# Where the value projections stand in a window-attention layer: between the q/k projections and the spread of the norms, with the five engines' orders set anew

## The reference, cut to what matters

```python
for i in range(6):
    x = attn_layer(shift_tokens(x), Wqkv[i], q_scale[i], k_scale[i], Wo[i]) + x
    x = ffn_layer(shift_tokens(x), ln_g[i], ln_b[i], W1[i], b1[i], W2[i], b2[i]) + x

def attn_layer(x, Wqkv, qs, ksc, Wo):        # 16 heads of 64
    q, k, v = split(x @ Wqkv)
    q, k = l2norm(q) * qs, l2norm(k) * ksc   # norm over the 64 features of a head
    q = q * cos * scale + rotate_half(q) * sin * scale
    k = k * cos / scale + rotate_half(k) * sin / scale
    # windows of 32 queries; keys and values of this window and the one before
    attn = softmax(8 * q k^T + mask)
    return (attn @ v) @ Wo
```

## Time and profile before

| | us |
|---|---|
| median of 3 runs | 2266.87 (2265.04 to 2267.53) |
| profiled execution, its time | 2274.98 |
| its span | 2273.2 |
| PE busy | 2019.9 (89%) |
| DVE busy | 1615.8 (71%) |
| ACT busy | 1093.3 (48%) |
| POOL busy | 891.1 (39%) |
| mean granted TensorE clock | 0.962 |

### The profile page before, as it was taken

The page is one execution under the profiler, slowest core; times in us unless marked ns, Lnnn a source line. Parts: engine busy times, 40 slices in busy tenths (PEclk is TensorE's granted clock), DMA queues, the critical chain, the costliest instruction groups (busy, mean ns, idle before and its releaser), DMA issues.

```text
span 2273.2 us, 84305 instructions
## 1 busy us (share of the span) xinstructions
PE 2019.9 (89%) x35280; PEld 1310.9 (58%) x35280; DVE 1615.8 (71%) x3316; ACT 1093.3 (48%) x1911; POOL 891.1 (39%) x1166
## 2 busy tenths in 40 slices
PE   6989896789998999979999799999799998899996
PEld 2333332466665666656666566766566765666664
DVE  5556645678876788866878677878687876777872
ACT  2333332355554555544555455646355654455553
POOL 0000001445544545443545353545354544444540
PEclk9999998899998999989999999999999998999996
DMA  1000100545555655454656455556465545555550
GB/s 58 5 9 5 51 0 11 82 80 81 83 88 100 93 82 84 78 101 84 95 82 89 98 85 81 91 84 87 86 104 79 91 82 94 89 89 81 83 87 25
DMA packets 72441, 168.15 MB, mean 74 GB/s; under 512 B 16496, under 2 KB 23408, under 8 KB 71408
## 3 DMA queue, kind: packets, MB, share of 16 engines
q0 software_dynamic: 36864, 100.71, 33.1%
q1 hardware_dynamic: 35456, 65.55, 11.1%
HBM read 20.45 MB, written 1.05 MB: 9 GB/s over the span
## 4 chain that ended last, share of the span: by engine, by line
PE 61%; DVE 15%; DMA 11%; issue 9%; POOL 2%; ACT 1%; SPq 1%; DVEq 0%; POOLq 0%; ACTq 0%
PE ps L922 13%; DMA big<-big 9%; PE ps L955 8%; PE ps L844 6%; PE ps L933 4%; PE ps L1009 4%; PE ps L992 4%; PE ps L979 3%; DVE big L743 3%; DVE big L740 3%; PE ps L1029 3%; PE ps L1022 3%; PE ps L1065 2%; POOL big L425 2%; PE ps L865 2%
## 5 line engine op out<-in xcount | busy, mean ns | idle before, releaser
L425 POOL DMA_DIRECT2D big<-big x768 | 607.5, 1494 | 93.7 <-DVE big L743 80.3
L922 PE MATMUL ps<-big,wn_sb 128*128 128x256 f32 x1536 | 404.7, 401 | 42.1 <-DMA wn_sb<-in_wn 22.2
L493 ACT ACTIVATE big<-ps 128x512 f32<-128x512 f32 x384 | 228.2, 597 | 399.7 <-PE ps L922 393.5
L922 PEld LDWEIGHTS ps<-big,wn_sb 128*128 128x128 f32 x1536 | 280.4, 195 | 119.8 <-issue 35.5
L751 DVE TENSOR_TENSOR big<-big,ps 128x512 f32<-128x512 f32 x384 | 243.7, 681 | 122.5 <-PE ps L945 81.9
L740 DVE TENSOR_TENSOR big<-ps,tab 128x512 f32<-128x512 f32 x384 | 258.5, 682 | 46.8 <-ACT big L493 46.8
L506 ACT ACTIVATE big<-ps 128x512 f32<-128x512 f32 x192 | 114.7, 597 | 358.9 <-PE ps L955 358.9
L756 DVE TENSOR_REDUCE top<-ps 128x8 f32<-128x512 f32 x192 | 123.3, 684 | 223.6 <-PE ps L979 223.6
L416 POOL TENSOR_TENSOR big<-big 128x512 f32<-128x512 f32 x96 | 121.8, 1269 | 357.8 <-ACT big L510 357.8
L743 DVE TENSOR_TENSOR big<-ps,tab 128x512 f32<-128x512 f32 x384 | 257.7, 681 | 0.0
L1065 PE MATMUL ps<-big,wo_sb 128*128 128x256 f32 x768 | 217.1, 386 | 1.9 <-issue 1.9
(11 more groups left out here) (146 smaller groups left out, 3119.9 us busy)
## 6 DMA issues: line engine op xcount, KB each, us to landing
big<-big POOLq DMA_DIRECT2D x768, 128.0 KB, 4.8
big<-big SPq DMA_DIRECT2D x96, 256.0 KB, 3.7
big<-big SPq DMA_DIRECT2D x96, 192.0 KB, 3.9
wn_sb<-in_wn SPq DMA_DIRECT2D x6, 1536.0 KB, 7.6
wo_sb<-in_wo SPq DMA_DIRECT2D x6, 512.0 KB, 5.2
w_sb<-in_w SPq DMA_DIRECT2D x6, 341.0 KB, 3.9
w_sb<-in_w SPq DMA_DIRECT2D x6, 192.0 KB, 4.9
big<-in_x SPq DMA_DIRECT2D x8, 128.0 KB, 2.2
```

What stands on the lines that cost most here:

```text
L425: eng.dma_start(rot[to:to + 32, at:at + 4, :], src[32 * r:32 * r + 32], accum_op=ALU.add).then_inc(added[i], 16)
L493: eng.activation(sq[:, two, :], ps[:, i % 2, :].rearrange("p (a t) -> p a t", a=2), ACT.Square).then_inc(sq_d, 1)
L922: mm = eng.matmul(ps[:, k % 2, a * T:a * T + T], wn_sb[:, u * P:u * P + P], sT, start=True, stop=True)
```

## The change

The four lists are replaced, and three waits follow the new use of banks 0 and 1: projections, values, spread norms. `V0` and `V1` now wait for `d6` and `d7`. `R0` waits for the copy `v2` (and, as before, for `N6`), `R1` for `v3`. The next iteration's `k0` waits for `H6` and `k1` for `H7`, in place of the wait for the copies. In the lists `k0` comes ahead of `S0`; `V0` to `V3` stand behind `W3`; on ACT the Gelu step `F4` comes ahead of `n0`, and `v0` to `v3` between `n0` and `F5`. The instructions that the program writes out are the same ones.

```diff
         PE_PLAN = [(x_[0], int(x_[1:])) for x_ in """
-            S0 k0 k1 F1 S1 k2 k3 T0 g0 T1 F2 k4 k5 W0 W1 g1 g2 k6 T2 k7 U0 T3 g3 W2 W3 U1 F4 O0 O1 O2 U2 O3 U3
-            F5 R0 R1 O4 R2 O5 R3 O6 R4 F6 R5 R6 O7 F7 R7 V0 V1 V2 V3""".split()]
+            k0 S0 k1 F1 k2 F2 S1 T0 k3 T1 k4 g0 g1 W0 W1 k5 T2 k6 T3 F4 k7 U0 U1 g2 g3 W2 W3 V0 V1 V2 V3 F5 O0
+            R0 O1 U2 R1 R2 O2 F6 U3 O3 O4 R3 R4 O5 F7 R5 R6 O6 O7 R7""".split()]
         ACT_PLAN = [(x_[0], int(x_[1:])) for x_ in """
-            s0 s1 x0 F1 s2 s3 t0 F2 t1 s4 s5 x1 s6 t2 s7 u0 t3 F3 n0 u1 F4 u2 u3 F5 v0 v1 v2 v3""".split()]
+            s0 F1 s1 s2 x0 F2 t0 s3 t1 x1 s4 s5 F3 t2 t3 s6 s7 F4 n0 v0 u0 v1 u1 v2 v3 F5 u2 u3""".split()]
         DVE_PLAN = [(x_[0], int(x_[1:])) for x_ in """
-            X0 X1 D0 D1 c0 c1 d0 d1 X2 X3 D2 c2 d2 c3 d3 D3 Z0 f0 c4 d4 c5 d5 f1 Y0 f2 c6 f3 Z1 n0 d6 c7 Y1 N1
-            d7 N2 N3 N4 N5 N6 H0 H1 H2 F5 H3 H4 F6 H5 H6 H7 F7 e0""".split()]
+            c0 d0 X0 X1 D0 D1 c1 c2 d1 d2 X2 D2 f0 X3 c3 D3 f1 d3 f2 c4 d4 f3 Z0 c5 d5 Y0 c6 d6 n0 c7 d7 N1 N2
+            N3 N4 Z1 N5 N6 Y1 H0 F5 H1 H2 F6 H3 H4 H5 H6 F7 e0 H7""".split()]
...
                         if isinstance(b, int) and b == 0:
                             eng.wait_ge(s_w, l * 16 + 16)
-                        if Bh:
-                            eng.wait_ge(vev, it * 4)
+                    if k < 2 and Bh:
+                        eng.wait_ge(hat_d, it * PAIRS + (k - 1))
...
                     if n < 2:
-                        eng.wait_ge(rot_d, it * PAIRS + (7 + n))
+                        eng.wait_ge(vev, it * 4 + (3 + n))
...
                     if j < 2:
-                        eng.wait_ge(hat_d, it * PAIRS + (7 + j))
+                        eng.wait_ge(rot_d, it * PAIRS + (7 + j))
```

## The result

The change makes the kernel slower: 2286.64 us in the median of 7 runs (2280.26 to 2298.46) against 2267.53 (2265.04 to 2274.25), a ratio of 1.0081 with a 95% interval of 1.0059 to 1.0103. The forecast was 2227. The profiled execution took 2281.36 us, with a span of 2279.6. It stands 5.3 us under the median, where the profiled one of the kernel before (2274.98) stands 7 us above its own: the two traces differ by 6.4 us, the medians by 19.1.

What follows compares the result with a forecast made beforehand. PE was taken to set the pace, 33.9 us of its own work in an iteration of 35.54. The profiled 2275.0 less 18 (46 iterations) and 22 (reload) gave 2235, or 2227 in the median; range 2198 to 2268.

Steps and rivals of the forecast that it cites:

- the block that moves: Walk from `W2 W3` through `V0` to `V3`: four table loads for two, `v0` ending at 23.3, `V2` waiting 0.7 us.
- Forecast steady iteration: One loop iteration taken as 35.15 us, a gain of 0.4; bounds a gain of 1.2 and a loss of 0.7.
- the transfers of `m3`: Accumulating transfer near the iteration's end: it lands by about 30 us after `k0` and holds up none.
- Walk of the new lists: Each engine stepped through its new list from `k0`, with costs from the profile: an iteration of 35.0 us.
- `V2`'s wait with one load: On PE, `V2` could start at 22.7 but waits 0.7 us for the copy `v0`, queued on ACT behind `n0`.
- Reload: Reload of `wn_sb` where a layer begins: PE's wait for it goes, 22 us in five places; bounds 0 and 30.
- two issue stalls at a layer's first steps: PE standing still some 3 us each where a layer begins, on code branched into there: both were to stay.
- The hole of 4.17 us in DVE before `X0`: DVE's largest idle time, while PE runs `V0` to `V3` and `S0`: it was to be gone.
- `R0` did not wait for `N6`: Sign that the forecast was wrong: `R0` waiting for `N6`, meaning 3.64 us of values fail to cover the norm chain.
- The end of the iteration, `H6` to `k0`: Last hand-over, DVE to PE: `H6` ends at 34.96, `k0` waits 0.3 us; over 0.8 would show the forecast wrong.
- the rival without cover at the end: DVE's tail and a new chain slip by 0.6 us each: period 36.2, 2285 profiled, 2277 median; chance 0.13.
- The rival with the dear switch of tables: A table switch on ACT costs 1.28 us beyond its load, delaying `V2`: 2293 profiled, 2285 median; chance 0.03.

Runs made afterwards that it cites:

- e1: Changed kernel with one named preload of the common logarithm and exponential table ahead of `n0`'s wait: 2211.46 us, 0.9725 of the kernel before; repeated, 2209.09 us, 0.9714.
- e2: Changed kernel with ACT's list reordered so that `n0`, `v0` and `v1` come ahead of `F4`, adding no table load: ratio 0.9754 to the kernel before.
- e4: Changed kernel with SP waiting for `H6` of a layer's last unit before it reloads the q/k/v weights: ratio 1.0155 to the kernel before.
- e7: Changed kernel with one table load more in an iteration, between `n0`'s square and `v0`: ratio 1.0408 to the kernel before.
- e6: Changed kernel with `V0` to `V3` back at the iteration's end, the old waits, and `n0` ahead of `F4` on ACT: ratio 1.0919 to the kernel before.

## Why the prediction was wrong

*The step that failed* is in the block that moves: "That makes four loads in an iteration for two", and with it "the load for `n0` runs to 21.5". There are five. The walk took it that one load serves `n0`. Left to the compiler, logarithm and exponential each brought a table of their own, and behind the load at L497 stands one at L499. The sign of it was in the code of before: `F5` asks for the common table by name, and between that and `n0`'s logarithm the list of before has no function of another table. So `v0` ended 24.84 us after `k0` and not 23.3, and `V2` waited 1.94 us and not 0.7. The Trainium skill, "ScalarE: Activation LUTs", section "Table sets: the hidden batching unit", counts a logarithm followed by an exponential as one load; the rows at L497 and L499 show two, and the measurement decides.

*What followed from it* was a second term that the prediction had at nothing: the clock. Its own waits were 0.7 us at most, and at that length no iteration is at the lower clock (e1: 35.03 to 35.07). At 1.94 us some are. That is 36.98 - 36.32 = 0.66 us in the mean of the steady iterations.

*The sizes.* Forecast steady iteration 35.15; measured 36.98, which is 1.83 more: 1.17 to the shortest, 36.32, with the second load in it, and 0.66 for the clock. Over 46 iterations the two are 84 us. Against the forecast of 2235 for the profiled execution that would make 2319; it took 2281.4. The other 38 us are in terms that went the other way. Around the layer starts the forecast with these two terms would be 20 x (1.83 - 0.39) - 22 = +7 us against before, and -13.0 was measured: 20 us. Of these, 12 are `V2`'s wait, which is 26.4 us in those 20 iterations where 20 x 1.94 = 38.8 would be, since part of it falls into stalls that stand anyway.

The first three iterations gained 10.1 where by the same sum they would have lost 3: 13 us. And the one iteration that I took as the measure of before, 35.54, was 0.37 shorter than the mean of the 24 steady ones, 35.91: 9 us. That too is a wait that the prediction under-counted: it said of the transfers of `m3` only that they hold up nothing in the new order, which is so, and took from one iteration that PE loses 1.6 us in the old one. Over the 24 it is 35.91 - 33.9 = 2.0, the rest being `R7` behind `H5` and its transfers. The prologue and the end took 3.9 us more. The kernel with the third load taken out ran at 2211 and 2209, 17 us under the forecast.

*The forecast's other points.* Walk of the new lists, 35.0 us: right, with some luck in the sum (35.03 with the load count that it assumed; `S1` at 5.63 for 5.6, `k7` at 16.6 for 16.4, `U0` 17.6 for 17.5, `V0` 21.0 for 20.9, these from the changed kernel). PE stood 0.59 us before `W0` and not 0.15, and with one table `R0` came at 26.95 for 26.5; the part from there to the next `k0` took 8.1 us for 8.5, so the two misses cancel. `V2`'s wait with one load, 0.7: 0.66.

Reload: the size was right, the sign to read it by was not. Handing the reload back cost 17 to 23 us for the 22 forecast. But there are still rows in which the projections wait for `wn_sb`: 5.3 us in two places in the changed kernel, and 21.5 in four places at the pace that the forecast had assumed, that of the kernel with one table. And of two issue stalls at a layer's first steps one was left, 3.85 us at the fourth layer for 3.07 and 3.43.

The loads are 138 more and not 96, 46 of them at L497. The hole of 4.17 us in DVE before `X0` is gone. `R0` did not wait for `N6`. The end of the iteration, `H6` to `k0`: a wait of 0.3 was expected and about that came, so the rival without cover at the end was wrong. The rival with the dear switch of tables came closest in time (2285 against 2286.64), by luck, and was wrong in its cause: behind each load on the way to `v0` the next instruction starts within 0.02 us, and 96 more of them elsewhere cost nothing. The kernel lost by the number of loads, not by their price.

*What stays open.* Why one wait of 1.94 us is followed by the lower clock and the same wait an iteration earlier is not; the rows show that the longer the wait, the more often it is, and no more. So the number of such iterations, 10 or 15 of 24 at the same wait, differs from run to run without a known reason, and the 19 us between the medians are explained by the traces only as far as their 6.4. Nor was it tried what makes up the 10 us that the first three iterations gained (5.9 of them are in the very first, 29.20 us for 35.11, where stage A runs alone).

## What to carry to other kernels

Before an activation is moved past another on its queue, write down which table each needs and which table the program asks for by name: a function moved across a Gelu can bring two loads, not one, when the compiler chooses, and a single named preload repairs it. Price a load by what is queued behind it: here 1.28 to 1.43 us each where PE waits for the copy behind it, nothing at 96 of them where ACT is idle. And when a walk through the lists says that a wait on PE grows from under one to two microseconds, add a term for the clock: here 0.66 us an iteration in the mean at a wait of 1.94. Take the pace of the kernel before from the mean of many iterations and not from one, when a wait for transfers is in it.

## What the runs showed of the hardware

- One table load is 1283 ns and the next instruction, where what it needs is there, starts within 0.04 us of its end, mostly 0.01, also three in a row (1168.79, 1170.08, 1171.37); that is so for 233 of the 236 in the changed kernel, and no drain shows, behind the load or ahead of it.
- The lower clock follows waits of PE that are shorter than the 3.07 to 3.43 us for which it stands still at a layer's start: one wait of 0.66 us in an iteration of 35 us never brought it (0 of 24, in both runs of that kernel), nor did one of 1.07 (`F5` in e2, 0 of 24). 1.94 us brought it in 10 of 24 iterations, and in 15 of 24 in e4; 3.36 us in 23 of 24 (e7), 3.58 us in 24 of 24 (e6, mean granted clock 0.96 in each). An iteration with it is 1.53 to 1.65 us longer than the shortest in the changed kernel and 1.3 to 1.7 in e7; the time goes in the steps right behind the wait, and in the pair of iterations compared above the steps from `O0` on are as long as without it.
- PE stands 0.59 us before `W0` in each iteration of all the new lists (0.15 was expected). The trace calls it "issue"; `D3`, which `W0` waits for, ends 0.32 us before it starts.
